# Reordering the seam of a four-layer token kernel: tile 0's small network before the last tile's second layer, and the last tile's contexts moved into rounds 2 to 5

## What is computed

```
x = x + [fc2(gelu(fc1(x))) | expert(gelu(fc1(x)))]     512 -> 2048 -> 384 + 128, one expert per sequence
x = x + x W_subject^T + b                              one 512x512 matrix per sequence
ctx    = causal_ema(x, tau_ctx)                        h = alpha*h + x along the 1024 tokens
gated  = x * sigmoid([x, ctx] Wg^T + bg)
mod    = 0.5 + sigmoid(gelu(x Wn1^T) Wn2^T + bn2)      4 values per token
temporal = sum over d of blend_d * causal_ema(gated * mod_d, tau_d)    4 time constants
out    = (gelu(x Wsoma^T) * sigmoid(temporal Wtemp^T)) Wout^T
x = x + layernorm(out)
x = x + x W_category + b                               one 512x512 matrix per sequence
```

## Time and profile before

| | |
|---|---|
| median of 3 runs | 1289.14 us |
| the profiled execution | 1290.09 us, of which the span is 1288.2 us |
| TensorE busy | 1273.0 us, 99% of the span |
| VectorE busy | 1065.2 us, 83% |
| ScalarE busy | 720.4 us, 56% |
| GpSimd busy | 78.9 us, 6% |
| chain that ended last | TensorE 86%, VectorE 8%, DMA 3% |
| DMA | 262.63 MB, mean 204 GB/s |
| granted TensorE clock | mean 0.997 of full |

### The profile page before, as it was taken

How to read it: one execution, slowest core, us unless ns; L and a number is a source line. 1 busy time by engine, 2 the same in 40 slices (tenths; PEclk the granted TensorE clock), 3 DMA queues, 4 the chain that set the end, 5 groups by cost and what they waited for, 6 DMA issues and landing times.

```text
span 1288.2 us, 17504 instructions
## 1 busy us (share of the span) xinstructions
PE 1273.0 (99%) x6109; PEld 1067.1 (83%) x6109; DVE 1065.2 (83%) x1682; ACT 720.4 (56%) x1369; POOL 78.9 (6%) x118
## 2 busy tenths in 40 slices
PE   8999999999999999999999999999999999999998
PEld 7788888888888888888887888778888888888877
DVE  7977777787786987777875699999999989998974
ACT  6577565776565875566864343543635353535344
POOL 0010000000000000000000111002100200020000
PEclk9999999999999999999999999989999999999999
DMA  8357554658744658645558898866456555654301
GB/s 291 102 170 236 185 179 131 221 164 266 217 167 151 230 179 264 208 148 171 198 187 273 303 327 327 329 254 220 173 220 238 211 182 208 249 201 160 131 17 66
DMA packets 114288, 262.63 MB, mean 204 GB/s; under 512 B 10345, under 2 KB 32873, under 8 KB 109081
## 3 DMA queue, kind: packets, MB, share of 16 engines
q1 hardware_dynamic: 94336, 183.27, 41.5%
q10 hardware_dynamic: 15032, 62.45, 13.9%
q0 software_dynamic: 4832, 15.79, 3.2%
HBM read 181.19 MB, written 80.28 MB: 203 GB/s over the span
## 4 chain that ended last, share of the span: by engine, by line
PE 86%; DVE 8%; DMA 3%; ACT 1%; issue 1%; ACTq 0%; DVEq 0%
PE bank L1593 29%; PE bank L1595 28%; PE bank L1594 28%; DVE drive L2304 2%; DMA x_slot<-x2hl_dram 1%; DVE drive L2293 1%; DVE temporal L2315 1%; DVE t_lo L2059 0%; DMA x_raw<-in_x 0%; DMA hb_in<-hb_dram 0%; DVE spikes_lo L2059 0%; DVE x_raw L2211 0%; DVE w_hl L2059 0%; DMA mod_t<-mod_dram 0%; PE bank L1901 0%
## 5 line engine op out<-in xcount | busy, mean ns | idle before, releaser
L1593 PE MATMUL bank<-h_hl,w_hl 128*128 128x512 f32 x512 | 199.5, 390 | 0.1
L1594 PE MATMUL bank<-h_hl,w_hl 128*128 128x512 f32 x512 | 199.3, 389 | 0.0
L1595 PE MATMUL bank<-h_hl,w_hl 128*128 128x512 f32 x512 | 199.2, 389 | 0.0
L1593 PE MATMUL bank<-t_hi,sp_hl 128*128 128x512 f32 x448 | 175.2, 391 | 4.4 <-DVE t_lo L2059 1.9
L1594 PE MATMUL bank<-t_lo,sp_hl 128*128 128x512 f32 x448 | 174.4, 389 | 0.0
L1595 PE MATMUL bank<-t_hi,sp_hl 128*128 128x512 f32 x448 | 174.4, 389 | 0.0
L1593 PEld LDWEIGHTS bank<-h_hl,w_hl 128*128 128x128 f32 x512 | 96.1, 188 | 20.8 <-issue 1.1
L1595 PEld LDWEIGHTS bank<-h_hl,w_hl 128*128 128x128 f32 x512 | 96.1, 188 | 20.0
L1594 PEld LDWEIGHTS bank<-h_hl,w_hl 128*128 128x128 f32 x512 | 96.1, 188 | 19.9
L1593 PEld LDWEIGHTS bank<-t_hi,sp_hl 128*128 128x128 f32 x448 | 84.1, 188 | 25.0 <-issue 1.8
L1595 PEld LDWEIGHTS bank<-t_hi,sp_hl 128*128 128x128 f32 x448 | 84.1, 188 | 17.6
(11 more groups left out here) (228 smaller groups left out, 3037.0 us busy)
## 6 DMA issues: line engine op xcount, KB each, us to landing
wg_hl<-wg_dram ACTq DMA_DIRECT2D x24, 1536.0 KB, 7.4
fc_raw<-in_fc_w SPq DMA_DIRECT2D x32, 512.0 KB, 4.2
hb_dram<-hb_out SPq DMA_DIRECT2D x64, 256.0 KB, 2.3
hb_in<-hb_dram ACTq DMA_DIRECT2D x64, 256.0 KB, 4.1
x2hl_dram<-x_hl POOLq DMA_DIRECT2D x28, 512.0 KB, 5.7
x_slot<-x2hl_dram SPq DMA_DIRECT2D x26, 512.0 KB, 5.1
wg_hl<-wg_dram SPq DMA_DIRECT2D x8, 1536.0 KB, 8.2
stage<-in_l_w SPq DMA_DIRECT2D x32, 256.0 KB, 3.4
```

The costliest lines, as they stand in the source:

```text
L1593: eng.matmul(ps, w_hi, x_hi, start=first, stop=False, skip_group_check=resumed)
L1594: eng.matmul(ps, w_hi, x_lo, start=False, stop=False, skip_group_check=resumed)
L1595: return eng.matmul(ps, w_lo, x_hi, start=False, stop=final, skip_group_check=resumed)
```

## The change

On TensorE `n1(0)` moves ahead of the last use of tile 6 and `mo(0)` ahead of use 0 (both now in bank 3, which use 0 writes once `mod` has been read). The gates of tile 0 follow uses 2, 4, 6 and 8 and no longer 4, 7, 9 and 11; the four `l1(6, m)` follow uses 2 and 3 in pairs. VectorE and ScalarE get a new order for the last tile's 16 uses. The contexts of tile 7 are no longer made in the seam, in place: each chunk is loaded again from `x2_dram` into a buffer of its own (`late_x`), one chunk in each of rounds 2 to 5, scanned, split and stored. SP and GpSimd follow.

```diff
+        late_x = place("late_x", 84, [TOK])
+        LATE = 7
+        LATE_UNITS = [(t, c) for t in range(LATE, NT) for c in range(KC)]
+        LATE_ROUND = 2
+        LATE_OF_ROUND = {r: LATE_UNITS[r - LATE_ROUND:r - LATE_ROUND + 1] for r in range(LATE_ROUND, LATE_ROUND + len(LATE_UNITS))}
...
         def n1_bank(i):
-            return bank[5 if i > 1 else 7]
+            return bank[5 if i > 1 else 7 if i else 3]
```

On SP, the late loads, the earlier loads of the first gate, and the store that is gone from the seam (its counterpart `store_late` stands in the rounds):

```diff
+            def load_late(t, c):
+                if late_no(t, c):
+                    on.wait_ge(s_ctxst, ctx_stored(LATE) + 16 * late_no(t, c))
+                else:
+                    on.wait_ge(s_x2lo, KC * LAST)
+                    on.wait_ge(s_x2st, 16 * NT)
+                    on.wait_ge(s_ctxst, ctx_stored(LATE))
+                eng.dma_start(late_x[:, :], x2_dram[t, :, c, :]).then_inc(s_xld[LAST % 2], 16)
...
+                if p == PAIRS - 1:
+                    load_wg(0)
+                    for c in range(KC):
+                        load_ctx(0, c)
                 store_hb(p, K8 - 1, 0)
...
+            load_xt(0, 0)
+            load_xt(0, 1)
             uses_done(1)
-            load_wg(0)
             pass_staged(PAIRS - 1, K8 + 2)
             uses_done(2)
-            for c in range(KC):
-                load_ctx(0, c)
+            store_ctx(LAST - 2, 1)
+            load_wg(1)
             uses_done(3)
+            load_wsoma(0)
+            load_wg(2)
...
-            store_ctx(LAST, 0)
-            store_ctx(LAST, 1)
             load_xt(2, 0)
```

On TensorE:

```diff
                 for v in range(13, HC):
+                    if p == PAIRS - 1 and v == HC - 1:
+                        n1(0)
                     fc2(2 * HC * p + v)
...
+                mo(0)
                 for j in range(HC):
                     fc2(2 * HC * p + HC + j)
-                    if j == 2:
-                        n1(0)
-                    if j == 3:
-                        mo(0)
-                    if j in (2, 3, 4, 5):
-                        l1(LAST - 1, j - 2)
-                    if j in (4, 7, 9, 11):
-                        gate(0, (4, 7, 9, 11).index(j))
+                    if j in (2, 4, 6, 8):
+                        gate(0, j // 2 - 1)
+                    if j in (2, 3):
+                        l1(LAST - 1, 2 * j - 4)
+                        l1(LAST - 1, 2 * j - 3)
```

On VectorE, the work that follows hb_lo and w2_lo of block j:

```diff
-                    if j in (5, 6, 7, 8):
-                        x2_of(t, j - 5)
-                    if j == 7:
+                    if j == 5:
                         gate_sum(0, 0)
                         traces_a(0, 0)
+                        x2_of(t, 0)
+                        x2_of(t, 1)
+                        traces_b(0, 0)
+                    if j == 6:
+                        x2_of(t, 2)
+                        traces_c(0, 0)
+                        x2_of(t, 3)
+                        traces_d(0, 0)
+                    if j == 7:
+                        for c in range(KC):
+                            x2_lo(t, c)
+                        gate_sum(0, 1)
+                        traces_a(0, 1)
                     if j == 8:
-                        traces_b(0, 0)
+                        traces_b(0, 1)
+                        context(t, 0)
                     if j == 9:
...
+                        traces_c(0, 1)
+                        traces_d(0, 1)
+                        context(t, 1)
                     if j == 10:
...
+                        gate_sum(0, 2)
+                        traces_a(0, 2)
+                        context(t, 2)
                     if j == 11:
...
+                        traces_b(0, 2)
+                        context(t, 3)
                     if j == 12:
...
+                        gate_sum(0, 3)
                         context_lo(t, 0)
                         context_lo(t, 1)
-                        traces_a(0, 2)
```

On VectorE in the seam:

```diff
-            context(LAST, 0)
-            context(LAST, 1)
             gate_sum(1, 1)
-            context(LAST, 2)
             spikes(0, 2)
-            context(LAST, 3)
             spikes(0, 3)
```

On VectorE in rounds 2 to 5:

```diff
                 spikes_low(r - 1, 2, 2)
+                for t, c in LATE_OF_ROUND.get(r, ())[:1]:
+                    context(t, c)
                 traces_a(r, 1)
...
                 traces_d(r, 1)
+                for t, c in LATE_OF_ROUND.get(r, ())[:1]:
+                    context_lo(t, c)
```

## The result

| | before | after |
|---|---|---|
| median, runs side by side | 1289.81 us (7 runs, 1289.02 to 1290.38) | 1294.53 us (7 runs, 1293.62 to 1295.80) |
| ratio | | 1.0038, interval 1.0027 to 1.0049 |
| profiled execution, span | 1290.09, 1288.2 | 1294.53, 1292.6 |

The forecast was 1293.1 in a range of 1287.0 to 1297.5, with slower at 0.55. Against the median of its own runs of before the loss is 4.7 us, where the sum said 3.9.

A forecast was written before the change was run, and what follows sets the result against it. TensorE, busy 99%, was taken as the bound, with only 7.6 us of idle and half clock in the seam to win. Terms 3.6 + 2.1 - 2.5 + 0.7 = +3.9 us on the 1289.14 median gave 1293.1, range 1287.0 to 1297.5.

The forecast's parts named there:

- term 1: Last tile's uses: VectorE's low parts come late, so TensorE waits 3.0 us at use 12 and 0.6 at use 14.
- rival, the clock falls there: At use 12's 3.0 us wait the clock falls to half rate, costing 3.4 us more: 1296.5 us, chance 0.14.
- term 2: Block 5's load, issued at about 700, lands after 7 us and delays gate_sum(0, 0): 2.1 us lost.
- term 3, the seam: Between last use and te(1): 1.4 us of context_lo leave VectorE's chain, te(1) starts at 854.4, 2.5 us won.
- term 4, round 2: Round 2: gate(2, 1) needs spikes(1, 0) from VectorE, 0.7 us given back; sumsq_lo just holds for ss(1).
- rounds 3 to 5: Each adds 1.5 us to VectorE, covered by its 1.62 us wait in round 3; rounds 4 and 5 taken alike.
- the rival on the side of faster: The seam closes: VectorE reaches the sums early enough, 7.6 us come back, 1285.1 us; chance 0.17.

The follow-up runs named there:

- one_scan: The changed kernel with one context scan moved from ahead of block 12's low parts to behind block 13's: 1293.04 us, ratio 1.0035.
- lows_first: The changed kernel with that scan behind block 13 and traces_b(0, 2) and traces_c(0, 2) behind block 15: 1290.66 us, ratio 1.0014.
- uses_only: The changed kernel's new order of the last tile's uses, with tile 7's contexts made in the seam again: 1293.57 us, ratio 1.0039.
- late_only: The kernel before with its order of uses kept, only tile 7's contexts moved to rounds 2 to 5: 1288.47 us, ratio 0.9996.
- late_r3: late_only with the late contexts in rounds 3 to 6: 1288.01 us, ratio 0.9989.
- lows_loads_r3: lows_loads with the four late contexts in rounds 3 to 6: 1288.81 us, ratio 0.9995.
- lows_loads: lows_first with SP issuing load_wg(4) after use 12 of the last tile, no longer after use 9: 1288.89 us, ratio 0.9999.
- split_te: late_r3 with te(1) computed in two halves of the contraction and temporal_low(1, 0) behind traces_a(1, 3): 1290.05 us, ratio 1.0001.
- sums_first: late_only with sum_squares(0) ahead of first_traces(1, 2) on VectorE: 1288.86 us, ratio 0.9996.

## Why the prediction came out right, and where it was wrong

| step | predicted | found |
|---|---|---|
| term 1, VectorE ahead of use 12 | 3.0 + 0.6 | waits of 3.1 (and 0.4 at use 14 where the clock held, with a stage A of +3.96) |
| rival, the clock falls there | 3.4, chance 0.14 | it fell, for half as long: 1.7 of work lost, 1.1 in stage A |
| term 2, block 5's load | +2.1 | 0 |
| term 3, the seam | -2.5 | -2.66 |
| term 4, round 2 | +0.7 | +1.75 |
| rounds 3 to 5 | 0 | 0 (all of stage D, rounds 3 to 7: -0.07) |

**Term 1** was right in place and size. The count of operations against TensorE's 32.0 us, with the four `x2_lo` ahead of gate_sum(0, 1), gave the 3.0 that the trace has as 3.11, and one_scan and lows_first show that it is VectorE's order. The two ends of the count are in the trace, gate(0, 1) on TensorE and gate_sum(0, 1) on VectorE:

```profile
720.55 0.28 PE L1613 MATMUL bank<-ctx_slot,wg_hl 128*128 128x256 f32 x1
```

```profile
725.95 0.69 DVE L2296 TENSOR_TENSOR bank<-bank,q_sb 128x512 f32<-128x512 f32 x1
```

gate_sum(0, 1) started 5.4 us after its gate, where the count had about 5.5, and the low part of block 12 was ready 29.9 us later, where it had 29.4. The 0.6 at use 14 did not appear in the changed kernel, since TensorE was slowed ahead of it; it was 0.37 in uses_only.

**Term 2** is the step that failed. It took the issue at "about 700" and a landing after 7 us, so that gate_sum(0, 0) would start near 708.9. ScalarE issued it at 697.95, and the data were there for the high part at 703.05, 5.1 us later. VectorE:

```profile
704.32 0.69 DVE L2080 TENSOR_TENSOR w_hl<-w_raw,w_hl 128x512 fp32r<-128x512 f32 x1
704.94 0.70 DVE L2296 TENSOR_TENSOR bank<-bank,q_sb 128x512 f32<-128x512 f32 x1
...
708.42 0.75 DVE L2238 SCALAR_TENSOR_TENSOR x_raw<-bank,l_b_sb,x_raw 128x512 f32<-128x512 f32 x1
```

gate_sum(0, 0) started at 704.94, 0.5 us after the 704.4 that the prediction has for a load in time, and nothing waited at 712 or 721. Of the 3.9 us by which the data came before 707, 2.05 are the issue and 1.9 the landing. By the prediction's own figures (2.1 us at a landing in 7 us, 4.4 at 9.4) the term is 0 once the data are some 2.2 us early, so the issue alone would have emptied it, as an estimate. Why this load landed in 5.1 us and those of blocks 2, 3 and 4, issued from 685.30 to 694.64, in 8.6, 7.0 and 6.7 is not shown. It was not that the queues were empty: the two loads of `xt` that SP issued at 688.3 and 688.8 took 10.8 to 12.3 us, GpSimd issued the two of `mod` while this one was under way, and from 698 to 702 us the DMA engines moved 371 to 412 GB/s.

```profile
699.89 1.11 POOL L991 DMA_DIRECT2D mod_t<-mod_dram  x2 [5.02 <-DMA mod_dram<-mod_row]
```

That a bulk load can hold up one of these small ones is true all the same: lows_first met it at block 13.

**The clock** was the rival at 0.14, and in the profiled execution it came true at half its price or less. The seven runs of the changed kernel had mean clocks of 0.996 and 0.997, the profiled one 0.997, so it is no outlier among them. In two profiles with use 12 waiting 3.1 and 2.99 us it fell once.

**Term 3** was right in its mechanism too: the scans that left the seam buy nothing, for VectorE idles ahead of spikes(0, 2) and spikes(0, 3), and the wait was cut into 2.90 and a second one: 1.15 at te(1) in the changed kernel, where the clock had fallen, and 0.97 at mo(2) with 1.74 at te(1) in late_only, where it had not. The prediction had 2.9 for the second. All eight versions without contexts in the seam and with te(1) whole have a stage B of 90.70 to 90.88, with the clock falling at ss(0) (after, late_r3, lows_loads_r3) or not.

**Term 4** took the giving-back as 0.7 at gate(2, 1) alone and let ss(1) "just hold". ss(1) held; VectorE's lateness came out one step further on, at mo(3), 0.84, where `h1_low` stands behind it. The term was mis-sized by 1.0.

**The sum** came out close by luck. Term by term, found less predicted: term 1 +0.4 (3.96 in uses_only, where the clock held), the clock +1.1, term 2 -2.1, term 3 -0.2, term 4 +1.0, rounds 3 to 7 -0.1. That is +0.2, from 3.9 to the 4.1 of the stages. With term 2 at the 0 that was found, the rest of the sum, +1.8, would have been 2.3 us too low.

The seam did not close, as said: the rival on the side of faster needed VectorE to be ahead there.

## What to carry to other kernels

Work moved earlier on an engine gains only if that engine does not have to wait for the bound engine before it is next needed; look for the first idle of that engine behind the place, since everything gained up to it is lost. What has no deadline (filters, scans) belongs behind what has one (the low parts of the next use), and a deferred step must be followed to the next deadline, not only past the first. A term that hangs on a load needs the time of its issue as well as its landing: here 2 us of the issue were the whole term. And cut two traces at instructions that both have: four numbers then say which part of a change costs what.

## What was not expected of the hardware

The fall of the clock is not tied to the length of the wait. TensorE stood idle for 2.90 us at ss(0) in eight profiles (2.89 in two of them): no stretch at half clock followed in late_only, one_scan, lows_first and lows_loads, 3.4 us in the changed kernel and in lows_loads_r3, 6.8 us in late_r3 and split_te; after 4.24 us it was 6.8 in the kernel before and 3.4 in uses_only. All of these stretches last 3.4 or 6.8 us. At mo(2) of sums_first an idle of 2.92 us was followed by 3.4 us at half clock, and at use 12 one of 3.11 by 3.4 us and one of 2.99 by none. At ss(0) a slow clock costs next to nothing, because without it te(1) waits for VectorE. Late_r3's 6.8 us at half clock left stage B at 90.80, against 90.74 in late_only without one. And of the 75 runs of the kernel before that were timed beside the experiments, the 35 with a mean clock of 0.997 took 1289.48 us in the mean and the 22 with 0.999 1289.62; the mean clock tells how long a run was slowed and not where. Of the 3.4 us that the prediction counted as lost to the clock before, little more than 1 could so be won back, as an estimate: te(1) started at 856.96, and the first half of temporal_lo was ready at 855.8. At use 12 less of it is covered: stage A is 91.85 with the fall and 90.72 without.
